# The second expert layer's loop of four steps, written out on TensorE, ScalarE and VectorE

## The chip, the core and the metric

The kernel runs on one core of a Trainium2 chip. The metric is the device time of one execution in microseconds (us). A core has five engines that run programs of their own and meet through semaphores: TensorE (PE; its weight loads are PEld), VectorE (DVE), ScalarE (ACT), GpSimd (POOL) and SyncE (SP, which here only issues transfers). Data moves by DMA queues over 16 DMA engines.

## What is computed

Two transformer blocks on x (4 x 1024 tokens, width 256), each with a cross attention over 77 context rows and a layer of eight experts, and gates on both. The change touches the last layer only, in which each expert picks its 256 tokens per batch element:

```python
def _L1_ffn_ref(x, gate_w, w_gate, w_up, w_down):
    k = S // E * CAPACITY                      # 1024 // 8 * 2 = 256
    affinity = softmax(x @ gate_w.T)           # (B, S, E)
    gating, idx = top_k(transpose(affinity), k)
    x_in = x[bidx, idx]
    h = silu(einsum('bekd,eid->beki', x_in, w_gate)) * einsum('bekd,eid->beki', x_in, w_up)
    x_e = einsum('beki,edi->bekd', h, w_down)  # inner width 1024
    return zeros_like(x).at[bidx, idx].add(gating[..., None] * x_e)
x = x + tanh(g_ffn[1]) * _L1_ffn_ref(_layernorm(x), ...)
```

## The kernel before

Each engine has one program that goes through the stages in turn: first attention, first expert layer, second attention, the choice of tokens (digit by digit of the gate values), second expert layer. All heavy products take their float32 operands as a high and a low float16 part, and `mm3` (L122 to L126) makes three matmuls of each product: high by high, low by high, high by low.

The second expert layer works on 16 items (NB1), one for each expert and pair of batch elements, with 512 rows each (BS). An item passes through a pipeline whose steps are written by `pipeline` (L87). In step j each engine does, in this order of code:

- TensorE (`ffn1_tensor`, L2051): `up` of item j-2, eight groups of twelve matmuls 128x512 into psG1 and psU1 (two buffers each); `transposes` of item j-1, eight into psXb; `down` of item j-3, 96 matmuls 128x256 into psYb.
- ScalarE (`ffn1_scalar`, L2102): silu of the eight groups and the high half of the hidden rows (hh), then the high half of the next rows (gxh), of the next up weights (upAh or upBh, in turn) and of the down weights (W1dh), then the results of item j-3 (yo).
- VectorE (`ffn1_vector`, L2164): the hidden rows (hid), their low half (hl), then the low halves of rows (gxl) and weights (upAl or upBl, W1dl). In steps 1 to 5 it also ends the choice of tokens for the second half of the batch.
- GpSimd: the adds of item j-3's results into out_x and the gather of new rows gx, four of each. SyncE: the loads of w1u (2 MB) and w1d (1 MB) for a later item. Both are written out in full.

The weights of the next item are thus split one step ahead, and the next load of w1u waits until VectorE has ended upAl or upBl.

`pipeline` writes the first depth + 1 = 6 steps (0 to 5) out one by one. What follows goes in a hardware loop (`e.Fori`) of `unroll` steps, as many turns as fit; the remainder is again written out. With 16 items and DD = 5 the loop of TensorE, ScalarE and VectorE has (16 - 6) // 4 = 2 turns of four steps: steps 6 to 9, one jump back, steps 10 to 13. Steps 14 to 19 follow in written-out code. `turns` is set to 0 by `straight=True`. In the loop, waits take their semaphore values from registers that depend on the turn; in written-out code they are constants.

The first expert layer uses `pipeline` too, with `unroll=2` and its own loop: 39 items, five steps ahead of the loop and 17 turns on TensorE. The second attention (L1599 to L1917) is written out in full.

Of the kernel before, what the change touches and what calls it, by code (L numbers as in the profile page):

```python
# [65 lines left out]
def wait(e, sem, value):  # L66

    if not isinstance(value, int) or value > 0:
        e.wait_ge(sem, value)
# [17 lines left out]
def pipeline(e, n, depth, work, unroll=2, straight=False):  # L87

    def step(j, phase):
        for lag, fn in work:
            item = j - lag
            if isinstance(item, int) and not 0 <= item < n:
                continue
            fn(item, (phase - lag) % unroll)

    first = depth + 1  # L100
    turns = (n - first) // unroll
    if turns < 2 or straight:
        turns = 0
    for j in range(min(first, n + depth - 1)):
        step(j, j % unroll)
    if turns:
        with e.Fori(0, turns) as u:
            for c in range(unroll):
                step(u * unroll + (first + c), (first + c) % unroll)
    for j in range(first + turns * unroll, n + depth - 1):  # L110
        step(j, j % unroll)
# [34 lines left out]
def program(nc, a, out, tab, n0_rows, x1_rows, n_rows):  # L146
    ctx = ExitStack()
    with ctx:
# [1280 lines left out]
        def read_at(q, p):  # L1429

            if p < DIGITS:
                return KSTEPS * q + SOFT + PASS * p + 3
            return KSTEPS * q + {THR: D_MASK, RANKS: D_MASK + 1, FILL: D_HOT + 1, TURN: KSTEPS}[p]
# [490 lines left out]
        NB1 = E * B // 2  # L1924
# [35 lines left out]
        DD = 5  # L1960
# [6 lines left out]
        def later(step, name):  # L1967

            return LATER.get((step, name)) if isinstance(step, int) else None
# [81 lines left out]
        def ffn1_tensor(pe):  # L2051
            def transposes(j, ph):
                par = ph % 2
                pe.wait_ge(d_in[par], 16 * NT * (j // 2) + 16 * NT)
                wait(pe, d_xl, KD * j)
                p = later(j + 1, "f5") if isinstance(j, int) else None
                if p is not None:
                    pe.wait_ge(k_dve, read_at(1, p))
                for k in range(KD):
                    for n in range(NT):  # L2060
                        last = pe.transpose(psXb[:, k, n * P:(n + 1) * P], gx[:, par, n, k * P:(k + 1) * P], ident[:])
                last.then_inc(d_xt, 1)

            def up(j, ph):
                par = ph % 2
                pe.wait_ge(d_xl, KD * j + KD)
                pe.wait_ge(d_wl, FT1 * j + FT1)
                for f in range(FT1):
                    wait(pe, d_hid, FT1 * j + (f - 1))
                    for psum, off in ((psG1, 0), (psU1, UP1)):  # L2070
                        for k in range(KD):
                            at = off + k * F1 + f * P
                            last = mm3(pe, psum[f % 2][:], W1uh[par][:, at:at + P], W1ul[par][:, at:at + P], gxh[:, par, k, :],
                                       gxl[:, par, k, :], k == 0, k == KD - 1)
                    last.then_inc(d_g, 1)
                    p = later(j + 2, f"f{f}") if isinstance(j, int) else None
                    if p is not None:
                        choose_pe(pe, 1, p, second0, second1)

            def down(j, ph):  # L2080
                par = ph % 2
                pe.wait_ge(d_hl, FT1 * j + FT1)
                pe.wait_ge(d_wdl, FT1 * j + FT1)
                for n in range(NT):
                    if n % 2 == 0:
                        wait(pe, d_yo, NT * (j - 1) + n + 2 if not isinstance(j, int) or j > 0 else 0)
                    rows = slice(n * P, (n + 1) * P)
                    for f in range(FT1):
                        at = f * D
                        last = mm3(pe, psYb[:, n, :], hh1[:, par, f, rows], hl1[:, par, f, rows], W1dh[:, par, at:at + D],  # L2090
                                   W1dl[:, par, at:at + D], f == 0, f == FT1 - 1)
                    if n % 2 == 1:
                        last.then_inc(d_y, 1)
                    p = later(j + 3, f"n{n}") if isinstance(j, int) else None
                    if p is not None:
                        pe.wait_ge(d_xl, KD * (j + 2) + KD)
                        choose_pe(pe, 1, p, second0, second1)
            for n in range(2):
                pe.wait_ge(c_exp[n], T)
            pipeline(pe, NB1, DD, [(2, up), (1, transposes), (3, down)], unroll=4)  # L2100

        def ffn1_scalar(act):  # L2102
            def up_high(f, early):
                def run(j, ph):
                    par = ph % 2
                    if isinstance(j, int) and j == 0 or (isinstance(j, int) and j == 1) != early:
                        return
                    if f == 0:
                        act.wait_ge(d_w[0], 16 * j + 16)
                        wait(act, d_g, FT1 * (j - 1))  # L2110
                    cols = slice(f * UC, (f + 1) * UC)
                    act.activation(W1uh[par][:, cols], w1u[:, cols], ACT.Copy, scale=SW).then_inc(d_wh, 1)
                return run

            def down_high(f):
                def run(j, ph):
                    par = ph % 2
                    if f == 0:
                        act.wait_ge(d_w[1], 16 * j + 16)
                        wait(act, d_y, 2 * (j - 1))  # L2120
                    cols = slice(f * DC1, (f + 1) * DC1)
                    act.activation(W1dh[:, par, cols], w1d[:, cols], ACT.Copy, scale=SW).then_inc(d_wdh, 1)
                return run

            def rows_high(j, ph):
                par = ph % 2
                act.wait_ge(d_xt, j + 1)
                wait(act, d_g, FT1 * (j - 1))
                for k in range(KD):
                    act.activation(gxh[:, par, k, :], psXb[:, k, :], ACT.Copy, scale=SX).then_inc(d_xh, 1)  # L2130

            def silu(f):
                def run(j, ph):
                    act.wait_ge(d_g, FT1 * j + (f + 1))
                    wait(act, d_hid, FT1 * j + (f - 1))
                    act.activation(sil1[:, f % 2, :], psG1[f % 2][:], ACT.Silu, scale=1.0 / (SX * SW)).then_inc(d_sil, 1)  # L2136
                return run

            def results(j, ph):
                par = ph % 2  # L2140
                if not isinstance(j, int) or j >= 2:
                    act.wait_ge(d_out[par], 16 * NT * (j // 2))
                act.wait_ge(d_gate, j + 1)
                for n in range(NT):
                    if n % 2 == 0:
                        act.wait_ge(d_y, 2 * j + (n // 2 + 1))
                    act.activation(yo1[:, par, n, :], psYb[:, n, :], ACT.Copy, scale=gsc[:, ph, n:n + 1]).then_inc(d_yo, 1)  # L2147

            def hidden_high(f):
                def run(j, ph):  # L2150
                    par = ph % 2
                    if f == 0:
                        wait(act, d_y, 2 * (j - 1))
                    act.wait_ge(d_hid, FT1 * j + (f + 1))
                    act.activation(hh1[:, par, f, :], hid1[:, f % 2, :], ACT.Copy).then_inc(d_hh, 1)  # L2155
                return run
            work = [(2, silu(0)), (1, up_high(0, True))]
            for f in range(1, FT1):
                work += [(2, silu(f)), (2, hidden_high(f - 1)), (1, up_high(f, True))]
            work += [(2, hidden_high(FT1 - 1)), (1, rows_high)]  # L2160
            work += [(1, up_high(f, False)) for f in range(FT1)] + [(2, down_high(f)) for f in range(FT1)]
            pipeline(act, NB1, DD, work + [(3, results)], unroll=4)

        def ffn1_vector(dve, ch):  # L2164
            def up_low(f, early):
# [55 lines left out]
            work = [(2, hidden(0)), (1, up_low(0, True))]  # L2221
# [2 lines left out]
            work += [(2, hidden_low(FT1 - 1)), (1, rows_low)]  # L2224
            work += [(1, up_low(f, False)) for f in range(FT1)]
            work += [(3, choose(3, "n1"))] + [(2, down_low(f)) for f in range(FT1)] + [(3, choose(3, "n2")), (3, choose(3, "n3"))]
            pipeline(dve, NB1, DD, work, unroll=4)

        with nc.Block() as block:
            @block.sync  # L2230
# [93 lines left out]
```

## Time and profile before

| | us |
|---|---|
| median of three timed runs | 1450.71 |
| lowest and highest | 1446.56, 1451.18 |
| the profiled execution | 1452.21 |
| its span, first to last instruction | 1450.5 |
| TensorE busy | 1317.3 (91%) |
| VectorE busy | 912.1 (63%) |
| ScalarE busy | 759.9 (52%) |
| GpSimd busy | 625.2 (43%) |

A row of a timeline has the start and the busy time of an instruction or of a merged group (x8 means eight of them), the engine, the line, the operation, the output and inputs by name, and in brackets how long the engine was idle before it and who released it. Lines of `mm3` appear as L124, L125 and L126 whoever calls it, so the tile names (psG, psU, psYb) tell the products apart. The granted clock (PEclk) is a share of TensorE's full speed.

### The profile page before, as it was taken

How to read it: one execution, taken by the hardware profiler on the slowest of the kernel's cores; microseconds unless marked ns; L12 is line 12 of the kernel's file. 1: busy time of each engine (PE TensorE's matmuls, PEld its weight loads, DVE VectorE, ACT ScalarE, POOL GpSimd, SP SyncE). 2: the span in 40 equal slices, each digit the busy share in tenths (PEclk: the TensorE clock that was granted, in tenths of full speed). 3: DMA queues.
4: the chain of work that ended last, by engine and by line, in shares of the span. 5: the costliest groups of instructions: out<-in, count | busy, mean ns of one | idle time of the engine just before them, and what ended most of it. 6: DMA issues, size and time to landing. Idle time of an engine off the chain costs nothing.

```text
span 1450.5 us, 29512 instructions
## 1 busy us (share of the span) xinstructions
PE 1317.3 (91%) x9858; PEld 988.9 (68%) x9859; DVE 912.1 (63%) x2123; ACT 759.9 (52%) x2313; POOL 625.2 (43%) x664
## 2 busy tenths in 40 slices
PE   6877699999999987999999965898999989999997
PEld 3766588889999856888888853355656646665555
DVE  2887664565554585778777855777655646655551
ACT  3765322433323365988878812444555646655552
POOL 2187777656666531554444413123233332233313
PEclk8665699999999989999999976999999999999998
DMA  5658445653333341000200102233333333444422
GB/s 145 215 146 201 76 50 70 134 87 62 61 65 61 52 124 59 23 31 31 95 31 30 33 29 76 102 117 117 117 117 117 117 118 117 123 159 158 130 44 30
DMA packets 81547, 133.20 MB, mean 92 GB/s; under 512 B 24662, under 2 KB 71260, under 8 KB 76316
## 3 DMA queue, kind: packets, MB, share of 16 engines
q1 hardware_dynamic: 51132, 93.92, 19.8%
q0 software_dynamic: 29312, 37.57, 15.6%
q8 instruction: 64, 1.05, 0.3%
q14 instruction: 47, 0.39, 0.1%
q10 hardware_dynamic: 992, 0.27, 0.1%
HBM read 95.08 MB, written 36.65 MB: 91 GB/s over the span
## 4 chain that ended last, share of the span: by engine, by line
PE 71%; DVE 10%; DMA 7%; issue 4%; POOL 4%; ACT 3%; SPq 1%; POOLq 0%; ACTq 0%; DVEq 0%
PE psG L124 5%; PE psG L125 5%; PE psG L126 5%; PE psU L124 5%; PE psU L126 5%; PE psU L125 5%; PE psYb L126 3%; PE psYb L124 3%; PE psYb L125 3%; DMA stage<-in_w 2%; PE psS L124 2%; PE psS L125 2%; PE psS L126 2%; PE psP L1747 2%; PE psOL L124 2%
## 5 line engine op out<-in xcount | busy, mean ns | idle before, releaser
L2045 POOL DMA_INDIRECT out_x<-yo,gidx x64 | 107.6, 1681 | 343.3 <-ACT yo L2147 327.3
L2196 DVE SCALAR_TENSOR_TENSOR hid<-psU,sil 128x512 f32<-128x512 f32 x128 | 88.4, 691 | 198.1 <-ACT sil L2136 197.8
L2136 ACT ACTIVATE sil<-psG 128x512 f32<-128x512 f32 x128 | 76.4, 597 | 217.5 <-PE psU L126 217.5
L980 POOL DMA_INDIRECT x_rows<-yo,tabs x78 | 124.4, 1594 | 94.9 <-ACT yo L1052 71.1
L1673 ACT ACTIVATE pr<-psS,mx 128x77 f32<-128x77 f32 x512 | 158.8, 359 | 0.8 <-DVE mx L1834 0.8
L125 PE MATMUL psYb<-W1dl,hh 128*128 128x256 f16 x512 | 140.4, 274 | 0.0
L124 PE MATMUL psYb<-W1dh,hh 128*128 128x256 f16 x512 | 140.4, 274 | 0.0
L126 PE MATMUL psYb<-W1dh,hl 128*128 128x256 f16 x512 | 140.3, 274 | 0.0
L1079 DVE SCALAR_TENSOR_TENSOR hid<-psU,sil 128x512 f32<-128x512 f32 x78 | 53.8, 690 | 127.7 <-ACT sil L1043 127.6
L1673 ACT ACTIVATION_READ_ACCUMULATOR pr<-psS,mx 128x1 f32 x512 | 123.7, 242 | 0.0
L1043 ACT ACTIVATE sil<-psG 128x512 f32<-128x512 f32 x78 | 46.5, 596 | 133.1 <-PE psU L126 133.1
L970 POOL DMA_INDIRECT bx<-n_rows,tabs x78 | 82.5, 1058 | 26.0 <-issue 21.9
L124 PE MATMUL psOL<-N,pt 128*128 128x256 f16 x320 | 89.2, 279 | 3.1 <-DVE pt L1817 3.1
L124 PE MATMUL psG<-bxh,Wh 128*128 128x256 f16 x312 | 85.6, 274 | 4.6 <-DVE bxl L1070 4.6
L2030 POOL DMA_INDIRECT gx<-n_rows,gidx x64 | 64.0, 1001 | 59.5 <-DVE gxl L2189 24.5
L125 PE MATMUL psOL<-N,pt 128*128 128x256 f16 x320 | 89.3, 279 | 0.0
L126 PE MATMUL psOL<-N,pt 128*128 128x256 f16 x320 | 89.2, 279 | 0.0
L2209 DVE TENSOR_TENSOR hl<-hid,hh 128x512 f16<-128x512 f32 x128 | 87.7, 685 | 1.7 <-ACT hh L2155 0.2
L124 PE MATMUL psU<-bxh,Wh 128*128 128x256 f16 x312 | 85.6, 274 | 0.0
L125 PE MATMUL psG<-bxl,Wh 128*128 128x256 f16 x312 | 85.6, 274 | 0.0
L126 PE MATMUL psU<-bxh,Wl 128*128 128x256 f16 x312 | 85.6, 274 | 0.0
L125 PE MATMUL psU<-bxl,Wh 128*128 128x256 f16 x312 | 85.6, 274 | 0.0
(403 smaller groups left out, 4189.5 us busy)
## 6 DMA issues: line engine op xcount, KB each, us to landing
w1u<-in_w SPq DMA_DIRECT2D x16, 2048.0 KB, 7.5
w1d<-in_w SPq DMA_DIRECT2D x16, 1024.0 KB, 8.1
stage<-in_w SPq DMA_DIRECT2D x8, 1536.0 KB, 8.7
X<-in_x SPq DMA_DIRECT2D x8, 512.0 KB, 8.9
n_rows<-xc SPq DMA_DIRECT2D x8, 512.0 KB, 9.5
x_rows<-X SPq DMA_DIRECT2D x8, 512.0 KB, 12.0
X<-x_rows SPq DMA_DIRECT2D x8, 512.0 KB, 8.1
out_x<-X SPq DMA_DIRECT2D x32, 128.0 KB, 1.7
```

What stands on the lines that cost most here:

```text
L124: pe.matmul(o, lh, rh, start=first, stop=False)
L125: pe.matmul(o, lh, rl, start=False, stop=False)
L126: return pe.matmul(o, ll, rh, start=False, stop=stop)
L970: pool.indirect_dma_start(bx[:, par, n, :], None, n0_rows[:, :], bass.IndirectOffsetOnAxis(tabs[:, j, n, 0:1], 0)).then_inc(b_in[par], 16)
L980: pool.indirect_dma_start(x1_rows[:, :], bass.IndirectOffsetOnAxis(tabs[:, j, n, 0:1], 0), yo[:, par, n, :], None, compute_op=ALU.add).the ...
L1079: dve.scalar_tensor_tensor(hid[:, half, :, :], psU[half][:, :, :], SH / (SX * SW), sil[:, half, :, :], ALU.mult, ALU.mult).then_inc(b_hid[ ...
L1673: ins = act.activation(pr1[:, par, h * LK:(h + 1) * LK], psS1[:, q, i * LK:(i + 1) * LK], ACT.Exp, bias=mx1[:, h:h + 1], scale=1.0 / (SX * ...
L2030: pool.indirect_dma_start(gx[:, j % 2, n, :], None, n_rows[0:2 * S * (j // E + 1), :], bass.IndirectOffsetOnAxis(gidx[:, half, col:col + 1 ...
L2045: pool.indirect_dma_start(out_rows[:, :], bass.IndirectOffsetOnAxis(gidx[:, half, col:col + 1], 0), yo1[:, j % 2, n, :], None, compute_op= ...
L2136: act.activation(sil1[:, f % 2, :], psG1[f % 2][:], ACT.Silu, scale=1.0 / (SX * SW)).then_inc(d_sil, 1)
L2196: dve.scalar_tensor_tensor(hid1[:, f % 2, :], psU1[f % 2][:], SH / (SX * SW), sil1[:, f % 2, :], ALU.mult, ALU.mult).then_inc(d_hid, 1)
L2209: dve.tensor_tensor(hl1[:, par, f, :], hid1[:, f % 2, :], hh1[:, par, f, :], ALU.subtract).then_inc(d_hl, 1)
```

## The change

The three calls of `pipeline` for the second expert layer, one on each of TensorE, ScalarE and VectorE, get `straight=True`. The loop of two turns is replaced by eight steps in a row. Order and number of the computing instructions stay the same on every engine; GpSimd and SyncE have the same program as before.

```diff
@@ ffn1_tensor
-            pipeline(pe, NB1, DD, [(2, up), (1, transposes), (3, down)], unroll=4)
+            pipeline(pe, NB1, DD, [(2, up), (1, transposes), (3, down)], unroll=4, straight=True)
@@ ffn1_scalar
-            pipeline(act, NB1, DD, work + [(3, results)], unroll=4)
+            pipeline(act, NB1, DD, work + [(3, results)], unroll=4, straight=True)
@@ ffn1_vector
-            pipeline(dve, NB1, DD, work, unroll=4)
+            pipeline(dve, NB1, DD, work, unroll=4, straight=True)
```

TensorE's program at the end of the loop's four steps, before. psYb are the down products of the last of them; a further pass starts at L107's branch, and what follows it here is step 14:

```order
5268 L124 MATMUL psYb<-W1dh,hh 128x256
5269 L125 MATMUL psYb<-W1dl,hh 128x256
5270 L126 MATMUL psYb<-W1dh,hl 128x256
5271 L107 REGISTER_ALU
5272 L107 COMPARE_AND_BRANCH
5273 L124 MATMUL psG<-gxh,upAh 128x512
5274 L125 MATMUL psG<-gxl,upAh 128x512
5275 L126 MATMUL psG<-gxh,upAl 128x512
```

The same place in the changed program, between steps 9 and 10:

```order
5214 L124 MATMUL psYb<-W1dh,hh 128x256
5215 L125 MATMUL psYb<-W1dl,hh 128x256
5216 L126 MATMUL psYb<-W1dh,hl 128x256
5217 L124 MATMUL psG<-gxh,upAh 128x512
5218 L125 MATMUL psG<-gxl,upAh 128x512
5219 L126 MATMUL psG<-gxh,upAl 128x512
```

The down products are followed at once by the next step's up products; the register instruction and the branch are gone, and TensorE's program has 6857 rows in place of 6141.

ScalarE's program at the same end of the four steps, before (W1dh is the down weights' high half, yo the results, sil the next step's silu):

```order
695 L2122 ACTIVATE W1dh<-w1d 128x256 x8
696 L2142 ISA
697 L2146 REGISTER_ALU
698 L2147 ACTIVATE yo<-psYb,gsc 128x256 x2
699 L2146 REGISTER_ALU
700 L2147 ACTIVATE yo<-psYb,gsc 128x256 x2
701 L107 REGISTER_ALU
702 L107 COMPARE_AND_BRANCH
703 L2136 ACTIVATE sil<-psG 128x512 x2
```

And in the changed program:

```order
683 L2122 ACTIVATE W1dh<-w1d 128x256 x8
684 L2147 ACTIVATE yo<-psYb,gsc 128x256 x4
685 L2136 ACTIVATE sil<-psG 128x512 x2
686 L2155 ACTIVATE hh<-hid 128x512
687 L2136 ACTIVATE sil<-psG 128x512
```

The computing instructions keep their order, and the register and wait instructions between them are gone with the branch.

## Rows read from the trace of the kernel before

**Rows 1.** The page: the chain that ended last, shares of the span by engine.
```profile
PE 71%; DVE 10%; DMA 7%; issue 4%; POOL 4%; ACT 3%; SPq 1%; POOLq 0%; ACTq 0%; DVEq 0%
```

**Rows 2.** Chain in order of time, 900 to 1451: start, us, what.
```profile
1122.79 0.87 PE psXb L2061 x8
1154.86 0.87 PE psXb L2061 x8
...
1194.75 0.87 PE psXb L2061 x8
...
1323.04 0.87 PE psXb L2061 x8
1355.11 0.87 PE psXb L2061 x8
```

**Rows 3.** TensorE by stretch: length, busy (matmul rows), granted clock, DMA share, GB/s.
```profile
1037.00:1166.00 129.00, 129.00 (x809) 1.00 0.43 132
1166.00:1171.00 5.00, 0.21 (x2) 0.88 0.99 415
1171.00:1177.00 6.00, 5.80 (x15) 0.53 1.02 252
...
1302.00:1432.00 130.00, 130.00 (x818) 1.00 0.37 106
```

**Rows 4.** Chain in order of time, 1160 to 1180.
```profile
1166.21 4.99 issue
...
1171.81 0.43 PE psG L125
...
1176.50 0.33 PE psG L124
1176.83 0.22 PE psG L125
```

**Rows 5.** Timelines of SyncE, ScalarE and VectorE, 1085 to 1200.
```profile
1131.57 0.33 SPq L1583 DMA_DIRECT2D w1u<-in_w  x1
...
1157.74 4.26 ACT L2112 ACTIVATE upAh<-w1u 128x512 f16<-128x512 f32 x8
1158.72 4.89 DVE L2172 SCALAR_TENSOR_TENSOR upAl<-w1u,upAh 128x512 f16<-128x512 f32 x8
1163.64 0.33 SPq L1583 DMA_DIRECT2D w1u<-in_w  x1
1166.25 0.84 ACT L2147 ACTIVATE yo<-psYb,gsc 128x256 f32<-128x256 f32 x2 [1.08 <-PE psYb L126]
```

**Rows 6.** Who waited for whom, 1030 to 1310: total us, times, longest.
```profile
DVE hid L2196 <- ACT sil L2136: 115.2, 66, 11.0
ACT sil L2136 <- PE psU L126: 112.3, 66, 9.5
...
PE psG L124 <- issue: 5.0, 1, 5.0
```

**Rows 7.** DMA queues in 270:490, 1040:1160, 1168:1170 (two), 1170:1181, 1181:1199, 1302:1440.
```profile
q8 instruction: 1, 0.02, 0.0%
...
q8 instruction: 6, 0.10, 0.3%
...
q1 hardware_dynamic: 52, 0.85, 101.4%
q8 instruction: 1, 0.02, 2.9%
...
q8 instruction: 2, 0.03, 1.3%
...
DMA packets 1, 0.00 MB, mean 0 GB/s; under 512 B 1, under 2 KB 1, under 8 KB 1
...
q8 instruction: 7, 0.11, 0.3%
```

**Rows 8.** TensorE by stretch in the first expert layer's loop, columns as in rows 3.
```profile
350.00:400.00 50.00, 50.00 (x460) 1.00 0.39 63
```

A queue's row has its packets, their MB and the share of the 16 DMA engines' time that they took.

## Prediction

> **What bounds the kernel now.** Start with the page. TensorE is busy for 91% of the span, and it holds 71% of the chain that ended last, more than all the others together [rows 1]. So the first question is whether the rewritten stretch belongs to TensorE, and where TensorE stands still in it.
>
> Next comes the chain of waits in order of time, from which I take one row for each step of the second expert layer, its eight transposes [rows 2]. Their starts give the length of a step. Inside the loop it is 1154.86 - 1122.79 = 32.07 us. After the loop, in code that is already written out, it is 1355.11 - 1323.04 = 32.07 us. The four steps from 1194.75 to 1323.04, with the loop's end among them, take 128.29 us, again 32.07 each. Only one step is different: 1154.86 to 1194.75 is 39.89 us. The loop has two passes of four steps (steps 6 to 9 and 10 to 13), and its one jump back lies in that step. It is **7.82 us longer** than its neighbours.
>
> The table of TensorE's busy time by stretch says the same [rows 3]: it is busy for all of 1037 to 1166, and all of 1302 to 1432, at a granted clock of 1.00 (the 2.4 GHz level). Between them, 1166 to 1171 has 0.21 us of work, and 1171 to 1177 runs at a mean clock of 0.53, nearly all of it at the 1.2 GHz level. The chain between 1177 and 1302 is told by the steps of [rows 2]. So the stage is TensorE's own time but for one hole.
>
> The chain around the hole [rows 4] gives its two parts. The last product of the first pass ends at 1166.21. Then stand 4.99 us of "issue", which means that TensorE waited for nothing that the profile shows. From 1171.20 on, the matmuls of 128x512 take 0.43 us each, where the later ones take 0.22.
>
> Do the other engines set the hole? No. At the first step of the second pass the up products need the split weights, whose last low part (upAl) ends at 1158.72 + 4.89 = 1163.61 [rows 5], 2.6 us before 1166.21. The list of waits of 1030 to 1310 [rows 6] has one wait of TensorE's matmuls ahead of psG, 5.0 us, and no engine named for it. ScalarE's longest wait for TensorE is 9.5 us there, VectorE's for ScalarE 11.0; without these, the other 65 of each average (112.3 - 9.5) / 65 = 1.6 and (115.2 - 11.0) / 65 = 1.6 us. Both engines are victims of the hole.
>
> **What the hole is.** The instruction queue q8 moves packets of 16 KB. In 1040 to 1160 there are 6 of them, one in 20 us; in 1302 to 1440, in written-out code, 7, again one in 20 us [rows 7]. That pace goes with TensorE's program. Around the jump it is broken: one packet lies in 1168 to 1170, right behind the jump, two more in 1170 to 1181, and in 1181 to 1199 one single packet of 0.00 MB moved in all, so none of q8. This reads as the refill of a store of code that the jump made useless: the first packet ends by 1170, TensorE starts at 1171.20, and two packets more restore the lead. The weights queue q1 takes 101.4% of the DMA time of 1168 to 1170, so the missing code moves while the load issued at 1163.64 and the one after it fill the DMA engines [rows 5, 7]. The first expert layer also has a TensorE loop, with 17 turns of two smaller steps. In 270 to 490 only one q8 packet moves [rows 7], and TensorE is busy 50.00 of the 50.00 us from 350 on [rows 8]. A loop whose code stays inside the store costs nothing that can be seen; this one does not stay.
>
> The Trainium skill, Runtime: NRT & Kernel Launch, section "Instruction fetch mechanics", says that a taken branch whose target is not held forces a fetch before execution goes on. By that rule, the trace agrees: one packet behind the jump and 4.99 us of idle. The same section has prefetch as purely sequential, which would leave the written-out code without such a stall.
>
> **The change part by part.**
> - *TensorE, removed:* the one jump back. Idle: 4.99 us. Clock: matmuls run at 0.43 instead of 0.22 us; from 1166.21 + 4.99 = 1171.20 to 1176.50 the chain spends 5.30 us on twelve matmuls that would take 12 x 0.22 = 2.64 us, and the thirteenth adds 0.33 - 0.22 = 0.11 us [rows 4]. That is 2.77 us, and 4.99 + 2.77 = 7.76 us, against 7.82 us by the rows of the steps, which I take. All of it is on the path, since TensorE has no other idle from 1037 to 1432.
> - *TensorE, also removed:* the entry branch and the register work ahead of each group. Steps inside the loop and outside it take the same 32.07 us, so these cost 0. The cover is TensorE's own queue of matmuls. The entry, just behind 1037, shows full busy time too [rows 3].
> - *TensorE, added:* 716 rows of code, which are not executed more often than before. The work per step stays. The cost is that of fetching new code in place of old; the first pass of the loop is new code too and is fetched at the same pace as the tail, so I take 0. Its bounds are given under the slower rival.
> - *ScalarE and VectorE:* each loses its jump and its register work. Both had ended their pass before TensorE did or just behind it (ScalarE's last result copy starts at 1166.25), and both wait 1.6 us a group on average [rows 6]. The first group of a step takes TensorE twelve matmuls, 2.6 us, so ScalarE is wanted at about 1168.8 and is free at 1166.25 + 0.84 = 1167.09: a cover of 1.7 us. Their own refill, if there is one, lies under the hole now. Gain 0. A jump left on them would need more than that cover to show; it goes with the same change.
> - *SyncE and GpSimd:* no instruction of theirs changes. Their issues after 1166 come 7.8 us earlier, in the same order.
>
> **What is late next when the hole goes.** The step head then looks like every other one, so the arrivals are those of the steps of 32.07 us. The nearest is the weights' low half, 2.6 us before TensorE needs it. The weight load issued at 1131.57 is split by ScalarE only from 1157.74 on, 26 us later, and the one issued at 1163.64 has the same 26 us to land [rows 5]. None becomes the bound, so nothing is given back.
>
> **The sum.** The profiled execution took 1452.21 us, 1.7 more than its span of 1450.5. 1452.21 - 7.8 = 1444.4. The median of the three timed runs is 1450.71, 1.5 us under the profiled one. Taken off that median: 1450.7 - 7.8 = **1442.9 us**, that is 0.54% less.
>
> The Trainium skill, Advanced Engine Details and Errata, section "Control Flow Timing", prices a compare-and-branch at about 108 ns. By that figure alone the change would be worth an estimated 0.1 us and the time would stay at 1450.6. The measured hole is 4.99 us, so the trace speaks for the fetch and against the bare price; the first rival below comes to the same time by a mechanism of its own.
>
> **Rivals.**
> 1. *The hole stays, or moves.* "Issue" only says that no cause is shown. If the 4.99 us come from the weight traffic holding up something else at that moment, written-out code has it too: 1450.7 us, no change. For it: q1 is at its full rate just then. Against it: the load at 1131.57 lies at the same place of its step [rows 5], and that step, 1122.79 to 1154.86, has no hole [rows 2]. Chance 7%.
> 2. *Only part returns.* The idle goes but something takes the clock's share, or ScalarE or VectorE arrive late at the first group. Then the gain is between 2.8 (the clock's part) and 5.0 us (the idle part): 1445.7 to 1447.9 us. Against it: with no idle there is nothing to lower the clock, which was 1.00 for 129 us up to the hole [rows 3]. Chance 8%.
> 3. *Slower: written-out code runs dry.* Each of the eight steps now needs new code, and a packet asked for during a burst of weights comes late. The price of one such stall is the measured one, 7.8 us. One of them cancels the gain (1450.7); from two on the kernel is slower: 1442.9 + 2 x 7.8 = 1458.5 us. It decides by TensorE's lead: the code held must be worth less than the burst of weights that delays a packet, which here runs from 1163.64 to beyond 1170. The rows speak against that. From 1181 to 1199 no q8 packet moves [rows 7] and the steps go on at 32.07 us [rows 2], so the store held at least 18 us of work; and the straight steps from 1302 on take one packet in 20 us at a DMA share of 0.37, without a hole [rows 3, 7]. Chance 4% for two or more. So the cost of one step of added code lies between 0 (it cannot gain, since TensorE is already busy throughout a straight step) and 7.8 us, and I take 0, by the nearest rows, the full busy time of 1302 to 1432 [rows 3].
>
> **Chances.** Forecast (1440 to 1446) 81%; part returned 8%; hole stays 7%; slower 4%. A measurement of this kernel can tell about 0.3%, or 4.4 us, from no change: the three runs of before spread from 1446.56 to 1451.18. The forecast lies 3.4 us beyond that line; so I count 4 of its 81 points as read inside it, and half of the partial case. Faster: 77 + 4 = 81%. Within: 4 + 4 + 7 = 15%. Slower: 4%. The range must hold the forecast with the spread of the runs (4.6 us) and, for the misses, the cases up to no change: 1437.5 to 1450.5.
>
> **What would show it.** In the profile after, transposes stand 32.07 us apart through the whole stretch, with no 39.9; the q8 packets keep one in 20 us with no cluster; no "issue" wait of 5 us stands on psG; the granted clock is 1.00 from about 1020 to the end; TensorE's busy time falls by some 2.8 us. I am wrong if a hole stands at a step head, if two or more stand elsewhere, or if the first sil group is late with TensorE not idle before it.

## The result, and the profile after

| | us |
|---|---|
| before, median of 11 runs | 1450.97 (1446.56 to 1452.56) |
| after, median of 11 runs | 1443.36 (1437.94 to 1445.4) |
| ratio, 95% interval | 0.995 (0.9936 to 0.9963) |
| profiled execution after, its span | 1441.8 |

The change saves 7.6 us, or 0.5%; by the interval of the ratio it is between 5.4 and 9.3 us. The forecast was 1442.9 us. The profiled execution's span is 8.7 us shorter than before.

The steps of the second expert layer, by their transposes, in the chain of the kernel after (start, us, what), answer to [rows 2]:

```profile
1025.30 0.91 PE psXb L2061 x8
...
1153.68 0.87 PE psXb L2061 x8
1185.76 0.87 PE psXb L2061 x8
...
1378.19 0.87 PE psXb L2061 x8
```

Steps 9 to 10, which took 39.89 us, now take 1185.76 - 1153.68 = 32.08. From the first to the last of these rows it is 352.89 us for eleven steps. Before, the same eleven ran from 1026.48 to 1387.19, the first and the last in this chain:

```profile
1026.48 0.91 PE psXb L2061 x8
...
1387.19 0.87 PE psXb L2061 x8
```

These are 360.71 us. The difference is **7.82 us**, the hole and nothing else. The remaining 0.9 us of the spans lie outside: the layer began 1.18 us earlier after the change (1025.30 against 1026.48), in code that did not change, and the stretch behind 1378.19 is 0.3 us longer than the one behind 1387.19.

TensorE by stretch after (length, busy, granted clock, DMA share, GB/s), against [rows 3]:

```profile
1037.00:1166.00 129.00, 129.00 (x805) 1.00 0.43 134
1166.00:1171.00 5.00, 5.00 (x25) 1.00 0.98 382
1171.00:1177.00 6.00, 6.00 (x30) 1.00 0.92 206
...
1302.00:1423.00 121.00, 121.00 (x775) 1.00 0.31 87
```

The weights' burst still fills the DMA engines at 1166 (0.98), but TensorE works through it at full clock. Who waited for whom after, in 1030 to 1302, against [rows 6]:

```profile
DVE hid L2196 <- ACT sil L2136: 108.7, 67, 3.2
ACT sil L2136 <- PE psU L126: 105.9, 67, 2.0
```

The longest wait of ScalarE fell from 9.5 to 2.0 us and that of VectorE from 11.0 to 3.2, and no row of issue ahead of TensorE's psG is left. The instruction queue after, in 1040 to 1160, 1160 to 1180 and 1180 to 1300, against [rows 7]:

```profile
q8 instruction: 6, 0.10, 0.3%
...
q8 instruction: 1, 0.02, 0.3%
...
q8 instruction: 6, 0.10, 0.3%
```

That is one packet in 20 us throughout; the cluster behind the jump is gone.

### The profile page after: what moved, and what is told of

It reads as the page before. It is cut to its first block, busy times and chain, and to the rows that moved or that the text cites. A ratio compares the mean times of both kernels' runs of the same rounds, so it can differ in the third digit from the quotient of the medians.

```text
span 1441.8 us, 29193 instructions
## 1 busy us (share of the span) xinstructions
PE 1303.8 (90%) x9858; PEld 980.8 (68%) x9859; DVE 911.7 (63%) x2123; ACT 760.3 (53%) x2313; POOL 625.9 (43%) x664
## 4 chain that ended last, share of the span: by engine, by line
PE 71%; DVE 11%; DMA 6%; issue 5%; POOL 4%; ACT 3%; SPq 1%; ACTq 0%; POOLq 0%; DVEq 0%
PE psG L124 5%; PE psG L125 5%; PE psG L126 5%; PE psU L124 5%; PE psU L125 5%; PE psU L126 5%; PE psYb L126 3%; PE psYb L124 3%; PE psYb L125 3%; DMA stage<-in_w 3%; PE psS L124 2%; PE psS L125 2%; PE psS L126 2%; PE psP L1747 2%; PE psOL L124 2%
## 5 line engine op out<-in xcount | busy, mean ns | idle before, releaser
L124 PE MATMUL psOL<-N,pt 128*128 128x256 f16 x320 | 88.2, 276 | 4.4 <-DVE pt L1817 4.4
L126 PE MATMUL psOL<-N,pt 128*128 128x256 f16 x320 | 88.3, 276 | 0.0
L125 PE MATMUL psOL<-N,pt 128*128 128x256 f16 x320 | 88.3, 276 | 0.0
L126 PE MATMUL psG<-bxh,Wl 128*128 128x256 f16 x312 | 85.6, 274 | 0.0
```

What stands on the lines that cost most here:

```text
L124: pe.matmul(o, lh, rh, start=first, stop=False)
L125: pe.matmul(o, lh, rl, start=False, stop=False)
L126: return pe.matmul(o, ll, rh, start=False, stop=stop)
```

## The experiments

The question was no longer whether the hole goes, but what it was: TensorE's jump alone, any jump, the code that is not held, or the weights' burst. The chips differed: the kernel before had a median of 1452.31 us beside the first four kernels and 1463.33 us beside the next four, so times are compared by the ratio to it. The row "after again" is the changed kernel once more, beside e5 to e7.

| | what | median, us | ratio, 95% interval |
|---|---|---|---|
| after | all three written out | 1443.36 | 0.995 (0.9936 to 0.9963) |
| e1 | TensorE alone written out | 1445.14 | 0.9948 (0.9936 to 0.996) |
| e2 | TensorE alone keeps its loop | 1450.44 | 0.9986 (0.9976 to 0.9997) |
| e3 | TensorE's loop has two steps | 1444.19 | 0.9937 (0.9916 to 0.9957) |
| e4 | before, small loads at the jump | 1446.83 | 0.9959 (0.9944 to 0.9974) |
| e5 | after, first layer's TensorE loop out | 1455.29 | 0.9942 (0.9921 to 0.9963) |
| e6 | after, extra traffic | 1454.81 | 0.9937 (0.9915 to 0.996) |
| e7 | after, first layer's loops out on four engines | 1456.94 | 0.9954 (0.9938 to 0.9969) |
| after again | with e5 to e7 | 1456.83 | 0.9954 (0.9937 to 0.9971) |

### e1: TensorE alone written out

```diff
-            pipeline(pe, NB1, DD, [(2, up), (1, transposes), (3, down)], unroll=4)
+            pipeline(pe, NB1, DD, [(2, up), (1, transposes), (3, down)], unroll=4, straight=True)
```

> Only TensorE's loop is written out; ScalarE and VectorE keep their loops of four steps. My theory: TensorE's refill is the whole hole, and a jump on ScalarE or VectorE has a cover of 1.7 us at the head of the step, so the step across the jump is 32.1 us (between 32.07 and 33), and the time is that of the changed kernel, about 1443.4 us. Rival: their own refill takes some 3 to 5 us like TensorE's. Then ScalarE's first sil of step 10 comes up to 3 us late, TensorE stands behind it for as long, the step is 33 to 36 us and the time 1444 to 1448 us.

The chain of e1 across the jump that ScalarE and VectorE still take:

```profile
1157.28 0.87 PE psXb L2061 x8
1189.36 0.87 PE psXb L2061 x8
```

32.08 us: no hole. ScalarE's timeline in e1 shows its own jump, between the results of step 9 and the first silu of step 10 (the bracket is its wait for TensorE), and below it the same place one step earlier, inside the loop, where it has no jump:

```profile
1168.67 0.84 ACT L2147 ACTIVATE yo<-psYb,gsc 128x256 f32<-128x256 f32 x2 [1.08 <-PE psYb L126]
1171.34 0.60 ACT L2136 ACTIVATE sil<-psG 128x512 f32<-128x512 f32 x1 [1.83 <-PE psU L126]
```

```profile
1136.60 0.84 ACT L2147 ACTIVATE yo<-psYb,gsc 128x256 f32<-128x256 f32 x2 [1.08 <-PE psYb L126]
1139.27 0.60 ACT L2136 ACTIVATE sil<-psG 128x512 f32<-128x512 f32 x1 [1.83 <-PE psU L126]
```

Across the jump, silu starts 1171.34 - 1168.67 = 2.67 us behind the results; without one it is 1139.27 - 1136.60 = 2.67 as well. So the jump itself costs ScalarE nothing that can be seen. In the first written-out step behind the loop it is 1299.56 - 1296.97 = 2.59: the loop's code costs 0.08 us in every step, jump or not, and the register work is the likely reason. The ratio is that of the full change. So writing out ScalarE and VectorE brings nothing that can be measured: **TensorE's loop is the whole of it**.

### e2: only TensorE keeps its loop

The reverse of e1: the change of the diff on ScalarE and VectorE, and none on TensorE.

> Only TensorE keeps its loop of four steps; ScalarE and VectorE are written out. My theory: the hole is TensorE's own, so it stays at about 5 us with the slow clock behind it, the step across the jump is 39.9 us and the time about 1451 us. Rival: the hole comes from ScalarE's or VectorE's jump, or from all three refills in one queue at the same moment. Then it shrinks clearly under 5 us, to a step of 32 to 37 us and a time of 1443 to 1448 us.

The chain of e2, in order of time:

```profile
1155.96 0.87 PE psXb L2061 x8
1195.10 0.87 PE psXb L2061 x8
```

and around the jump:

```profile
1167.31 5.01 issue
1172.33 0.60 PE psG L124
1172.93 0.43 PE psG L125
...
1176.33 0.21 PE psU L124
```

The idle is 5.01 us against 4.99 before, so neither ScalarE's nor VectorE's jump has a part in it. The step takes 39.14 us instead of 39.89. The slow clock ended earlier after the restart: nine matmuls, 1176.33 - 1172.33 = 4.00 us, until the first fast one. Before, twelve took 5.30 us and the thirteenth, with 0.33 us, was still partly slow [rows 4]. So the clock's part of the hole varies between executions while the idle does not. The ratio, 0.9986, is 2 us short of no change. In the profiled execution 0.75 us are this shorter stretch; the rest is not explained.

### e3: a loop of two steps on TensorE

```diff
-            pipeline(pe, NB1, DD, [(2, up), (1, transposes), (3, down)], unroll=4, straight=True)
+            pipeline(pe, NB1, DD, [(2, up), (1, transposes), (3, down)], unroll=2)
```

> TensorE has a loop of two steps in place of four, so five turns and four jumps back; the other engines are written out. My theory: what costs is code that is no longer held. A body of two steps is half as long, and if it stays held (as in the first expert layer, whose loop of two smaller steps moves one packet in 220 us) there is no hole at any of four jumps, the steps are 32.07 us throughout, the instruction queue goes nearly silent in the loop and the time is about 1443.4 us. Rival: every taken jump costs its 4.99 us of idle and the clock, whatever is held. Then there are four steps of 39.9 us and the time is 1443.4 + 4 x 7.8 = 1474.6 us.

This is the run that tells a jump from a jump to code that is no longer held. TensorE by stretch in e3:

```profile
1037.00:1100.00 63.00, 63.00 (x392) 1.00 0.44 134
1100.00:1160.00 60.00, 60.00 (x364) 1.00 0.45 141
1160.00:1300.00 140.00, 140.00 (x898) 1.00 0.42 131
```

Four jumps back and not one hole; each step takes 32.07 us. The DMA queues of e3 in 1160 to 1340, and then in 1340 to 1400:

```profile
q1 hardware_dynamic: 1728, 18.88, 27.8%
q0 software_dynamic: 4464, 5.99, 16.5%
q14 instruction: 5, 0.04, 0.1%
...
q8 instruction: 2, 0.03, 0.2%
```

In 180 us of the loop, q8 has no row at all, where written-out code moves a packet in 20 us. It comes back when the loop has ended. So the body was held, q8 is TensorE's code, and a jump back into held code costs nothing. An estimate from the pace of a packet in 20 us: two steps of 32.07 us are 3.2 packets of 16 KB and four steps are 6.4. The first amount stays held and the second does not. Where between them the bound lies was not tried. The loop of two steps is also as fast as the written-out code, as far as the intervals tell, and TensorE's program holds 6 + 2 + 4 = 12 steps of code against 20.

### e4: small weight loads at the jump

```diff
+            cols = 64 if j == 9 else WU
-            sp.dma_start(w1u[:], a["w1"][j % E][:, 0:WU]).then_inc(d_w[0], 16)
+            sp.dma_start(w1u[:, 0:cols], a["w1"][j % E][:, 0:cols]).then_inc(d_w[0], 16)
```

and the same for w1d at j == 8, in the kernel before.

> The kernel before with its loops, but the two weight loads around the jump (w1u for item 9 and w1d for item 8) move 64 columns each instead of the full 2 MB and 1 MB, so two items are computed with partly stale weights. My theory: the hole is the fetch of code behind the jump, made longer by the loads that fill the DMA engines at that moment. Without them it shrinks from 5.0 to about 2 to 3 us but does not vanish. The clock may then stay up, and the step across the jump is 34 to 37 us, the time 1446 to 1449 us. Rival one: the weight traffic itself makes the hole. Then it is gone, the step is 32.07 us and the time 1443.4 us. Rival two: the fetch does not feel the loads: 4.99 us and a step of 39.9 us as before.

The chain of e4 around the jump:

```profile
1166.67 0.11 PE psYb L126
1166.78 1.94 issue
1168.72 0.39 PE psG L124
1169.11 0.22 PE psG L125
```

With the DMA engines nearly empty the idle is 1.94 us instead of 4.99, and the clock stays up: from the second one on, matmuls take 0.22 us. The first takes 0.39, so 0.17 us of a restart are not the clock's. The step across the jump is 34.18 us (1155.43 to 1189.61), so the hole costs 2.1 us in place of 7.8. The weights' burst thus makes 3.05 us of the idle, and with the shorter idle the slow clock did not follow either; the 1.94 us remain without the burst. The queues say how. In the kernel before, 1168.0 to 1168.5:

```profile
q1 hardware_dynamic: 12, 0.20, 92.4%
q8 instruction: 1, 0.02, 11.5%
```

In e4, 1165.5 to 1166.0:

```profile
q8 instruction: 1, 0.02, 11.5%
q1 hardware_dynamic: 2, 0.00, 0.3%
```

Windows of 0.1 us put the starts closer. Before, the packet starts in 1168.4 to 1168.5, at least 2.1 us behind the last matmul of the pass (1166.21) and under the burst; in e4 it starts in 1165.9 to 1166.0, at least 0.7 us ahead of it (1166.78). From there to the restart it is 2.7 to 2.8 us both times (to 1171.20 and to 1168.72), and in e2 as well (1169.5 to 1169.6, restart 1172.33). So it is the start of this packet that the burst delays, by some 3 us, and not what follows.

This packet has a forerunner that the prediction's windows left out. Before, 1162.2 to 1162.3, and e4, 1162.7 to 1162.8:

```profile
q8 instruction: 1, 0.02, 69.9%
```

```profile
q8 instruction: 1, 0.02, 67.2%
```

Both start about 4.0 us ahead of the last matmul, and so do those of e2 and e8. From it to the next packet it is 6.2 us under the burst and 3.2 without, so the whole delay lies between these two. Whether the forerunner is the last packet of the old pace or already belongs to the jump is not shown: no row shows the branch itself, nor what a packet holds. That TensorE's packets move before the last matmuls have run fits an instruction side that runs ahead of the array.

### e5 and e7: the first expert layer written out too

```diff
-            pipeline(pe, NB0, BDEPTH, [(2, up(0)), (1, transposes), (2, up(1)), (3, down)])
+            pipeline(pe, NB0, BDEPTH, [(2, up(0)), (1, transposes), (2, up(1)), (3, down)], straight=True)
```

e5 has this on top of the change; e7 has it on all four engines with a loop there.

> The changed kernel, and TensorE's loop in the first expert layer (17 turns of two steps) written out as well. My theory: that loop's code stays held, so its 16 jumps back cost nothing, and writing it out gives nothing: the time stays at that of the changed kernel, 1443 to 1444 us, while the instruction queue q8 now moves a packet every 10 to 25 us in 310 to 490. Rival: each of the 16 jumps hides a small stall that the modelled ends of the matmuls cover, say 0.1 us or more. Then the layer's stretch gets 1.6 us or more shorter and the time falls to 1442 us or less.

> The changed kernel, and the loops of the first expert layer written out on TensorE, ScalarE, VectorE and SyncE. My theory: the same as for TensorE alone: nothing was lost at those jumps, so 1443 to 1444 us. Rival: register work and jumps of ScalarE, VectorE or SyncE (the table loads) stand somewhere on the path of the first layer: then it is 1 to 5 us faster than the changed kernel, 1438 to 1442 us.

The chip of these runs is slower for all kernels, so the yardstick is the changed kernel run beside them.

> The changed kernel once more, on the chip of these runs, as their yardstick: 0.995 of the kernel before, so about 1444 us, with all steps of the layer at 32.07 us.

It came to 1456.83 us, 0.9954 of before. e5 has 1455.29 and e7 1456.94 us. Neither can be told from it: the intervals overlap for the most part. But e5 lies 1.5 us under it, and the rival of e5 forecast 1.6, so the times alone do not decide. In 310 to 490 the instruction queue of e5 does move code:

```profile
q8 instruction: 17, 0.28, 0.6%
```

A packet in 10.6 us, where the changed kernel has none of q8 there. The length of the steps decides. From the chains, one row of transposes for each item, e5 and then the changed kernel (after again):

```profile
378.28 0.44 PE psX L999 x4
...
502.73 0.44 PE psX L999 x4
```

```profile
377.01 0.44 PE psX L999 x4
...
501.46 0.44 PE psX L999 x4
```

Both are 124.45 us for fifteen steps, 8.30 each, with seven jumps back among them in the second. A stall of 0.1 us at each jump would have made the second 0.7 us or more longer. The reading of [rows 8] holds: jumps back into a held body were worth nothing that can be seen, and so is their removal. For the other three engines of e7 only the times speak, and they would not show a gain under some 3 us. Twice the code rate of the second layer also does no harm.

### e6: extra traffic in the written-out layer

```diff
                 load_down(sp, j)
+                if j >= 4:
+                    sp.wait_ge(s_keep, 16 * (NG + j - 4))
+                    sp.dma_start(spare_rows, a["w1"][j % E][:, 0:4096]).then_inc(s_keep, 16)
```

The definition of `spare_rows` and a wait at the end of SyncE's program are left out here.

> The changed kernel, and in the second expert layer one more copy of 2 MB from memory to memory in each step from item 4 on, right behind the weight loads. It has no use in the computation. It makes the burst that delays the code about twice as long. My theory: written-out code has a lead of at least 18 us, so TensorE still never runs dry: no wait of issue in front of psG or psYb, steps of 32.07 us, about 1444 us. The slower rival of the prediction: a packet asked for in such a burst comes too late; then holes of 1 to 5 us stand in several of the steps, the steps are 33 to 40 us and the time is over 1450 us.

TensorE over eleven steps of e6:

```profile
1040.00:1390.00 350.00, 350.00 (x2184) 1.00 0.57 198
```

The DMA share over the layer is 0.57 where the kernel after has 0.42 in 350 us (1030 to 1380), and TensorE is busy all the time. Its steps are 32.07 us. So the slower rival of the prediction does not begin at this load either. From which load on it would, was not tried.

### e8: more traffic at the jump

```diff
                     load_up(sp, j + 1)
+                if j == 8:
+                    sp.dma_start(n0_rows[0:2048, :].rearrange("(p r) d -> p (r d)", p=P), a["w1"][j % E][:, 0:4096]).then_inc(s_keep, 16)
                 load_down(sp, j)
```

A wait at the end of SyncE's program is left out here.

> The kernel before with its loops, and one useless copy of 2 MB from memory to memory issued between the w1u and the w1d load just ahead of the jump back. My theory: the code behind the jump moves among the loads, so more traffic delays it further: the idle grows from 4.99 us to 6 us or more (it was 1.94 us with hardly any load), and the step across the jump from 39.9 to 41 us or more. Rival: the share of the engines that the code gets is the same under any full load, and the idle stays at 5.0 us and the step at 39.9 us.

One run, 1454.86 us beside one of 1451.91 for the kernel before, on the same chip: the times decide nothing here, and the reading rests on one trace. The chain of e8:

```profile
1168.89 4.89 issue
1173.78 0.61 PE psG L124
...
1179.08 0.43 PE psG L124
1179.51 0.24 PE psG L125
```

My expectation failed and the rival held: the idle is 4.89 us and the step 39.90 (1157.54 to 1197.44). The queues of e8 in 1171.0 to 1171.5 show the packet:

```profile
q1 hardware_dynamic: 13, 0.21, 99.3%
q8 instruction: 1, 0.02, 11.5%
```

It starts at least 2.1 us behind the last matmul (1171.0 - 1168.89), as before, although 2 MB more are queued. So full DMA engines delay the code by about 3 us, and another 2 MB behind the load did not add to it.

## Why the prediction was right

- **What bounds the stage.** Right. TensorE alone, by the steps and the table by stretch; taking its hole away left 32.07 us everywhere.
- **What the hole is.** Right, and now shown and not only read off: it needs TensorE's loop (e1, e2), it vanishes if the body is held (e3), and it is not made by the traffic, since 1.94 us of it remain without (e4). Rival 1 gave the traffic as the whole cause; it is a part, 3 us of the idle and the way to the slow clock. The prediction had the fetch as one cause and put no size on the traffic's part. It also read one packet as the answer to the jump; there was another 4.0 us ahead of the last matmul, in 1160 to 1168, which its windows skipped.
- **The sum.** The term of TensorE was 7.82 us and the steps gave back 7.82 us. The medians give 7.6, and their interval of 5.4 to 9.3 us would not tell 7.8 from 6 or 9; that 1442.9 came within 0.5 us of 1443.36 is partly luck, with runs that spread over 7.5 us. The split into 4.99 idle and 2.8 clock was nearly right for that execution (0.17 us of the 2.8 come at full clock too, by e4), but e2 shows that the second part is not fixed: its slow stretch was 4.00 us long instead of 5.30.
- **ScalarE and VectorE at 0.** Right, and the cover of 1.7 us was not needed for it: ScalarE's step head is 2.67 us with the jump and 2.67 without (e1). No refill of theirs was seen.
- **The added code at 0.** Right, even with more traffic (e6) and with twice the code rate (e5).
- **What would show it.** Steps, queue pace, clock and waits came as listed. One item was wrong in size: TensorE's busy time was to fall by 2.8 us and fell from 1317.3 to 1303.8, by 13.5. Most of the rest is not of this change. In 0 to 300, whose code is the same, the executions before and after differ by 7.9 us. Columns: length, busy of PE, PEld, DVE, ACT, POOL, clock, DMA share, GB/s; before, then after:

```profile
0.00:300.00 300.00, 244.71 (x1915) 202.64 (x1917) 192.07 (x611) 139.04 (x281) 180.40 (x180) 0.79 0.57 131
```

```profile
0.00:300.00 300.00, 236.82 (x1906) 196.39 (x1908) 191.03 (x610) 138.76 (x281) 179.15 (x180) 0.81 0.56 131
```

  The granted clock differs there (0.79 and 0.81), and a busy time at half clock counts double while the engine waits for others anyway. The busy total of a whole execution was the wrong thing to predict a gain of 8 us by; the distance between two rows of the same step was the right one.
- **The range.** It was 13 us wide, since it also had to hold the misses; the runs after the change spread over 7.5 us.

## What to carry to other kernels

When one step of a steady pipeline is longer than its neighbours and TensorE's idle there has no releaser, look for a jump back at that place and at the instruction queue: here silence in the loop meant that the body was held and the jump was free; packets throughout the loop, with a cluster at the jump, meant that it was not. The remedy is either to write the loop out or to shorten its body until it stays held; here two steps in place of four did as well. Only TensorE, which sets the end here, needed it, and the jump cost most where bulk loads were issued at the same point (4.99 us of idle against 1.94).

## What the runs showed of the hardware

- A jump back of TensorE into code that has to be fetched cost 1.94 us of idle with quiet DMA engines and 4.89 to 5.01 us with full ones. Another 2 MB in the queue did not lengthen it (one trace).
- The idle of 1.94 us left the clock at its full level (granted clock 1.00); those of 4.89 to 5.01 us were followed by 4.0 to 5.7 us at the 1.2 GHz level.
- From the start of the last code packet before the restart to TensorE's first matmul it was 2.7 to 2.8 us, with full DMA engines and with quiet ones.
- A body worth an estimated 3.2 packets of 16 KB stayed held, one worth 6.4 did not.
- Behind the jump TensorE ran for 18 us (1181 to 1199) without a packet of code, so at least that much was held ahead; and with a DMA share of 0.57 over the layer, written-out code was never late.
